# One register load for four tiles' expert numbers, and an earlier placing with scatters spread over the last sample

## The reference

```
s = _L0_attn_ref(xn, W_Q, b_Q, W_K, b_K, W_V, b_V, W_O, b_O, ln1_w, ln1_b, ln2_w, ln2_b)
g = _silu(_L0_ffn_ref(xn, Wr, br, W1, b1, g1, be1, W2, b2))   # router, top 2 of 16,
x = x + s * g                     # per expert: gelu(layernorm(h W1 + b1) g1 + be1) W2 + b2
```

## Time and profile before

| | |
|---|---|
| median of 3 runs | 1665.83 us |
| profiled execution | 1672.02 us |
| its span (first to last instruction) | 1670.1 us |
| busy in the span | PE 1285.4, DVE 1070.8, ACT 724.9, POOL 600.8 us |
| layer 0's attention, about | 42 to 567 us |
| its last sample, steps 0 to 31 | 426 to 561 us |
| its experts, about | 569 to 665 us |

### The profile page before, as it was taken

The page is one execution under the profiler, slowest core; times in us unless marked ns, Lnnn a source line. Parts: engine busy times, 40 slices in busy tenths (PEclk is TensorE's granted clock), DMA queues, the critical chain, the costliest instruction groups (busy, mean ns, idle before and its releaser), DMA issues. The chain is left out here.

```text
span 1670.1 us, 21792 instructions
## 1 busy us (share of the span) xinstructions
PE 1285.4 (77%) x7188; PEld 869.9 (52%) x7188; DVE 1070.8 (64%) x2574; ACT 724.9 (43%) x1526; POOL 600.8 (36%) x597
## 2 busy tenths in 40 slices
PE   1799999998987777376677985785784886788885
PEld 0355554654644555254564663553563465566664
DVE  1366676778686343455655995996897699724334
ACT  1345555455443234123236653662672573343332
POOL 1243444343338422422311442343243144225551
PEclk9998999999988678677778897797897799799998
DMA  7200000000000112430000000000000000001113
GB/s 176 71 1 1 1 1 2 1 1 1 1 4 29 51 51 70 129 111 13 13 1 1 1 1 0 1 1 0 1 1 1 1 1 1 26 12 34 35 33 89
DMA packets 54315, 40.36 MB, mean 24 GB/s; under 512 B 13175, under 2 KB 46685, under 8 KB 54205
## 3 DMA queue, kind: packets, MB, share of 16 engines
q1 hardware_dynamic: 35516, 23.91, 4.9%
q0 software_dynamic: 4544, 9.32, 2.0%
q10 hardware_dynamic: 14146, 5.75, 1.6%
HBM read 25.92 MB, written 13.04 MB: 23 GB/s over the span
## 5 line engine op out<-in xcount | busy, mean ns | idle before, releaser
L753 POOL TENSOR_TENSOR PR<-PR,R 128x256 f32<-128x256 f32 (+3 forms) x128 | 161.5, 1262 | 280.8 <-DVE R L1205 276.3
L1617 POOL TENSOR_TENSOR SA<-SA,H 128x512 f32<-128x512 f32 x64 | 81.8, 1277 | 258.2 <-DVE H L1844 258.2
L1839 DVE TENSOR_TENSOR_SCAN H<-DAS,H 128x512 f32<-128x512 f32 x128 | 174.6, 1402 | 0.0
L1022 ACT ACTIVATE PR<-banks,NM 128x129 f32<-128x129 f32 (+3 forms) x256 | 132.6, 527 | 47.5 <-DVE NM L1182 45.0
L415 PE MATMUL banks<-BCR,identR 96*128 96x512 f32 x256 | 110.7, 519 | 54.5 <-DVE H L1844 45.6
L415 PEld LDWEIGHTS banks<-we,HH 128*128 128x128 f32 x1024 | 145.3, 211 | 10.4
L415 PE MATMUL banks<-we,HH 128*128 128x128 f32 x1024 | 144.5, 294 | 0.0
L415 PEld LDWEIGHTS banks<-PTS,V 128*64 128x64 f32 x1280 | 72.9, 143 | 103.4 <-issue 97.1
L415 PE MATMUL banks<-XNT,we 128*128 128x512 f32 x256 | 120.7, 594 | 0.0
L415 PE MATMUL banks<-PTS,V 128*64 128x128 f32 x1280 | 105.0, 295 | 19.6 <-DVE PTS L1190 12.6
L1190 DVE COPY PTS<-banks 128x128 f32<-128x128 f32 (+3 forms) x128 | 62.2, 486 | 86.8 <-PE banks L893 83.8
(11 more groups left out here) (512 smaller groups left out, 2700.2 us busy)
## 6 DMA issues: line engine op xcount, KB each, us to landing
xsort<-zrow SPq DMA_DIRECT2D x1, 3072.0 KB, 13.1
XS<-xsort SPq DMA_DIRECT2D x12, 256.0 KB, 2.9
ysort<-PTS SPq DMA_DIRECT2D x12, 256.0 KB, 2.2
pj_stage<-in_L_ffn_w_proj SPq DMA_DIRECT2D x1, 2048.0 KB, 10.2
we<-in_L_ffn_we SPq DMA_DIRECT2D x1, 2048.0 KB, 9.3
we<-yrows SPq DMA_DIRECT2D x8, 256.0 KB, 4.9
X<-in_L_attn_resid_pre ACTq DMA_DIRECT2D x4, 256.0 KB, 4.7
xrows<-XN SPq DMA_DIRECT2D x4, 256.0 KB, 2.3
```

What stands on the lines that cost most here:

```text
L753: nc.gpsimd.tensor_tensor(p, p, R[:, n, :].unsqueeze(2).to_broadcast([P, 2, w]), ALU.mult).then_inc(pn, 1)
L1022: nc.scalar.activation(PR0[:, q % 2, s, OFF[t]:OFF[t] + w], ps2(n)[:, s, 0:w], ACT.Exp, bias=NM[:, n, s:s + 1], accum_out=L[:, n, s:s + 1] ...
L1617: nc.gpsimd.tensor_tensor(Y[m], Y[m], H[:, n % 2, m, :], ALU.add).then_inc(ya, 1)
L1839: nc.vector.tensor_tensor_scan(H[:, n % 2, m, :], DA[:, n % 4, m, :], H[:, n % 2, m, :], 0.0, ALU.mult, ALU.add).then_inc(scn, 1)
```

## The change

Three things, all in layer 0:

1. VectorE packs the four expert numbers of a unit into one integer (number i times 16 to the power i, summed), and TensorE loads this one per unit and takes each number out by shift and mask.
2. In the last sample "rank" comes first (step 1), "cc" at step 3, the four "o" at steps 5 to 11, "sel" at step 17. The placing parts 7 to 12 run at steps 3, 4, 6, 7, 9 and 11. The four parts of the output norm move three steps later (13, 14, 19, 20).
3. The 32 scatters are issued in steps 12 to 31, one or two each, instead of two in each of steps 16 to 31.

```
                     u = 2 * (i // T) + t // 2
                     key = None
-                    if u == 0 and b:
+                    if b == B - 1:
+                        if u == 0:
+                            key = ("rank",)
+                        elif u == 1:
+                            key = ("cc", b - 1)
+                        elif u < 6:
+                            key = ("o", b - 1, u - 2)
+                        elif u == 8:
+                            key = ("sel",)
+                    elif u == 0 and b:
                         key = ("cc", b - 1)
...
-                            if b and i == 11:
+                            late = 3 * (b == B - 1)
+                            if b and i == 11 + late:
                                 out_scale(b - 1)
-                            if b and i == 17:
+                            if b and i == 17 + late:
                                 out_norm(b - 1)
-                            if b == B - 1 and i >= 16:
-                                scatter(2 * (i - 16))
-                                scatter(2 * (i - 16) + 1)
+                            if b == B - 1 and i >= 12:
+                                for k in range(32 * (i - 12) // 20, 32 * (i - 11) // 20):
+                                    scatter(k)
...
+                                packed = nc.tensor.value_load(TEI[0:1, u:u + 1], min_val=0, max_val=E ** 4 - 1)
                                 for i in range(4):
-                                    e = nc.tensor.value_load(TEI[0:1, 4 * u + i:4 * u + i + 1], min_val=0, max_val=E - 1)
+                                    e = (packed >> (4 * i)) & (E - 1)
...
-                                nc.vector.tensor_scalar(TEI[:, :], TEF[:, :], float(E - 1), None, ALU.min).then_inc(el, 1)
+                                link(nc.vector.tensor_scalar(TEF[:, :], TEF[:, :], float(E - 1), None, ALU.min))
+                                link(nc.vector.tensor_tensor(TEP[:, :].rearrange("o (g i) -> o g i", i=4),
+                                                             TEF[:, :].rearrange("o (g i) -> o g i", i=4),
+                                                             radix[:, :].unsqueeze(1).to_broadcast([1, NF, 4]), ALU.mult))
+                                link(nc.vector.reduce_sum(TEF[:, 0:NF], TEP[:, :].rearrange("o (g i) -> o g i", i=4), AX.X))
+                                nc.vector.tensor_copy(TEI[:, :], TEF[:, 0:NF]).then_inc(el, 1)
 
-                        PLACE_AT = {12: (7,), 13: (8,), 14: (9,), 15: (10,), 16: (11,), 17: (12,)}
+                        PLACE_AT = {3: (7,), 4: (8,), 6: (9,), 7: (10,), 9: (11,), 11: (12,)}
...
+                        for i in range(4):
+                            last = nc.vector.memset(radix[:, i:i + 1], float(E ** i))
+                        link(last)
...
-                                if i == 10:
+                                late = 3 * (b == B - 1)
+                                if i == 10 + late:
                                     out_stats(b - 1)
-                                if i == 16:
+                                if i == 16 + late:
                                     out_apply(b - 1)
```

More of the change, by code:

```diff
@@ L603, in layer0 @@
                         key = ("w1", u - 1)
-                    elif b == B - 1:
-                        key = {5: ("rank",), 10: ("sel",)}.get(u)
                     elif u == 5:
@@ L665, in layer0 @@
                 TEF = sbr("TEF0", [1, 4 * NF], c=c)
-                TEI = sbr("TEI0", [1, 4 * NF], I32, c=c)
+                TEP = sbr("TEP0", [1, 4 * NF], c=c)
+                radix = sbr("radix0", [1, 4], c=c)
+                TEI = sbr("TEI0", [1, NF], I32, c=c)
                 EC = sbr("EC0", [E, 4], c=c)
```

## The result

The changed kernel takes 1637.2 us (median of 4 runs, 1635.88 to 1638.29) where the kernel before takes 1664.1 (1661.51 to 1669.95): a ratio of 0.9833, 95% interval 0.9804 to 0.9862. The forecast was 1640. The profiled execution has a time of 1637.49 us and a span of 1635.7, against 1672.0 and 1670.1 before. The profile of before is thus 7.9 us above the median of its runs and that of the changed kernel 0.3 us: the two profiles differ by 34.5 us, the medians by 26.9.

What follows compares the result with a forecast made beforehand. Bounds: TensorE early in the last sample, then VectorE's placing and GpSimd's scatters; in the experts, the cross-engine chain. Terms -17.3, +4.8 and -13.6 sum to -26.1: 1645.9 us profiled, 1640 median; own range 1631 to 1649, overall 1629 to 1658.

Steps and rivals of the forecast that it cites:

- Experts, forecast -17.3: Layer 0's expert layer, twelve units of four tiles: one load per unit saves 17.3 us, bounds 0 and -21.
- The pitch of the hidden products: Expert layer, time per tile's hidden product at full clock: falls from 0.76 to 0.27 to 0.30 us.
- The mean of the two clock levels: Expert layer: half the time at each clock level, periods 4.7 and 5.5 us, so 5.2 taken.
- The rival that register work is as dear as the loads: Expert layer: pitch stays at 0.7 or so, set by the number of register instructions; 1657 us, chance 0.09.
- chain close over another wait: Expert layer: ScalarE's in-order copies bind, period falls only to 6 us; -9 instead of -17.3, 1648 us, within a 0.15 case.
- A to C, forecast +4.8: Last sample, steps 0 to 11 in groups of four: early placing and ranks add 4.8 us, bounds 0 and +10.
- The new wait for "cc": Last sample, step 3: turned shares come later, VectorE waits with row maximum 3 queued behind; about 1.5 us.
- the slower rival: Last sample, steps 0 to 11: TensorE idles, its clock falls to the lower level; 1674 us, chance 0.05.
- D to H, forecast -13.6: Last sample, steps 12 to 31 in groups of four: 75.3 us against 88.9, bounds 0 and -19.
- GpSimd's need, as forecast: Last sample, steps 12 to 31: GpSimd's work per four-step group at 1.24 us a scatter, 11.3 to 16.4 us.
- The yardstick of 13.15 for a group: Sample 1 group with only two V products as spares, 13.15 us; over it steps 12 to 31 lose 23.1 us.
- The rival in which the early groups eat the scatters' gain: Last sample: steps 0 to 11 stretch by 10 us, later ones give 9; 1648 or 1649 us, within a 0.15 case.

Runs made afterwards that it cites:

- no_registers: Changed kernel with expert weights from fixed places, no register load, shifts, masks or address work (output differs): 1616.9 us, 0.9738 of the kernel before.
- load_only: Kernel before with the packed expert numbers alone (one load per unit), old order of the last sample: 1648.5 us, 0.9888 of the kernel before.
- cc_first: Changed kernel with turned first-row shares at step 1, ranks at step 3, placing parts 7, 8 and 10 a step later: 1630.0 us, 0.9824 of before.
- all_four: Changed kernel with load ahead of the waits, HN before statistics, scatters from step 8, and turned shares ahead of the ranks: 1611.5 us, 0.9718 of before.
- scatters_late: Changed kernel with two scatters in each of steps 16 to 31, as before the change: 1642.5 us, 0.9848 of the kernel before.
- all_three: Changed kernel with load ahead of the waits, HN before statistics, and scatters from step 8: 1612.8 us, 0.9719 of the kernel before.
- order_only: Changed kernel with one load per tile again and no packing, so only the last sample's order is new: 1658.1 us, 0.9941 of the kernel before.
- norm_late: Kernel before with only the four parts of the output norm three steps later in the last sample: 1666.5 us, 0.9985 of the kernel before.
- after_again: The changed kernel itself, unaltered, measured once more beside the last version on the same chip: 1632.7 us, 0.9839 of the kernel before.
- norm_first: Changed kernel with VectorE making HN of unit g-2 before the statistics of unit g-1: 1621.0 us, 0.9763 of the kernel before.

## Why the prediction was right, by its own steps

**Experts, forecast -17.3, measured -17.6.** The sum holds, and its parts too: nine periods 13.3 forecast, 13.5 measured; units 0, 1 and the last 4.0 forecast, 4.1 measured (35.0 to 30.9). But the period of 5.19 came out near the forecast's 5.2 by two errors that cancel. *The pitch of the hidden products* was the mis-sized term: 0.27 to 0.30 was forecast, four products 1.1 us; they take 1.47 at full clock. Shift and mask aren't free as the single address instruction of the earlier trace rows is; no_registers, with neither, has 1.13 us. So the full-clock period is 5.05, not 4.7. *The mean of the two clock levels* was the other: half of the time at each was read from a clock of 0.74, but the clock rose to 0.89, and six of the nine periods had full-clock products (6 x 5.05 + 5.35 + 5.51 + 5.52 = 46.7). Had it stayed, the period would have been (5.05 + 5.5) / 2 = 5.3 and this term 12.4 to 12.6.

The rival that register work is as dear as the loads is false: load_only has 78.4 us in the experts where before has 95.1. Nor did the chain close over another wait at 6 us a period. What was missed in this part is the bigger thing. The prediction took 1.05 us from HN to products as "semaphore, one load and register work" and kept it as given. It is 0.62 us of load that can stand ahead of the wait. The chain was read rightly, and a link of it was not questioned.

**A to C, forecast +4.8, measured +4.2.** A +1.86 and B +1.65 against 2 each, C +0.7. The new wait for "cc" is there:

```profile
437.47 0.17 DVE L1224 TENSOR_TENSOR CC<-PR,R 128x6 f32<-128x6 f32 x1 [1.48 <-PE banks L415]
...
440.28 1.92 PE L415 MATMUL banks<-X1T,WQ 128*128 128x512 f32 x2 [1.72 <-DVE G L1153]
...
443.27 1.62 DVE L1270 TENSOR_SCALAR CNT<-CNT 128x16 f32<-128x16 f32 x1
```

VectorE waits 1.48 us (forecast 1.5); cc_first, which takes it away, gives 1.9, though all_four got only 0.3 out of the same order. The rest of the sum is right by terms that are not: VectorE's busy time came out at 12.2, 14.4 and 12.8 us in A to C, where 14.2, 14.7 and 11.8 were forecast, so that A grew by 1.9 us with less work and more waiting than reckoned. The second row is the slower rival's mechanism, a TensorE that has idled and a product of 1.92 us: it occurs once in A, whose clock is 0.92, and B has 0.97, C 1.00; it never falls below the 0.9 named as the sign against. The third row is the small operation beside a GpSimd multiplication, 1.62 us for what takes 0.17 alone. The prediction took such a stall to be in part 7; it is in part 8 now. The four new small operations lie at 474.4 to 475.2, 0.7 us of VectorE, as forecast.

**D to H, forecast -13.6, measured -15.3.**

| | D | E | F | G | H |
|---|---|---|---|---|---|
| forecast | 13.4 | 15.4 | 17.6 | 15.2 | 13.7 |
| measured | 14.8 | 13.8 | 16.3 | 15.5 | 13.2 |
| GpSimd's need, as forecast | 11.3 | 13.7 | 16.4 | 13.7 | 12.5 |

The need at 1.24 us a scatter is what E and F take (13.8, 16.3), with nothing above it; the 1.2 to 1.7 that the forecast put on top there were not paid. D fails in the other direction, and scatters_late shows why: there a scatter costs by its place in the step, not by the engine's free time. G is 1.8 over its need with a granted clock of 0.83. In all_three G takes 12.1 us, at full clock and with three scatters fewer.

The yardstick of 13.15 for a group was too high. D of scatters_late, with the square-root step of the norm and some spares, takes 11.99, so the sum lost over it was underestimated. The rival in which the early groups eat the scatters' gain had +10 and -9 us; with +4.2 and -15.3 it is out.

**The signs named.** Period of 4.7 to 5.5: yes. A and B longer by 2: 1.9 and 1.7. First scatter at about 482: 479. E at 15 to 16: 13.8, better. A pitch of 0.27 without queue idle: no, 0.37. GpSimd never waiting 4 us for VectorE: true from the first scatter on, where the longest wait is 2.97. Ahead of that no: in A to C it waits up to 5.94 us, as it did before, with nothing else to do.

**The sum.** -26.1 forecast for the profiled execution, -34.5 measured between the two profiles, -27 between the medians. The stretches that the forecast spoke of give -28.6. The other 5.9 lie in the layers after, whose code is the same, and the prediction had put 0 there. So the profiled execution was missed by 8.4 us (1645.9 against 1637.5), and that the 1640 still came within 3 us of the median is in part luck: the prediction took off 6.2 us because the profile of before lay that far above the median of its first three runs, and the profile of the changed kernel lies only 0.3 above its own.

What the 5.9 us are stays open. One block of the first products after the experts, in before, in the changed kernel, and in the changed kernel measured again:

```profile
696.45 5.24 PE L415 MATMUL banks<-QK 128*128 128x512 f32 x8
```
```profile
666.93 3.70 PE L415 MATMUL banks<-QK 128*128 128x512 f32 x8
```
```profile
665.31 5.87 PE L415 MATMUL banks<-QK 128*128 128x512 f32 x8
```

Between the first two profiles the block and the two ahead of it, at a higher clock, make 2.6 of the 5.9 us. But the third has the changed kernel's code and before's slow block, so this difference is of the execution and not of the change. Over all of the layers after the experts a difference is left even so: the three profiles with a load per tile (before, order_only, norm_late) have 1004.9 to 1005.9 us, all eleven others 996.0 to 1001.9 (after_again 998.5). On one chip that ran both kinds it is 1004.9 twice against 1001.5 and 1001.9. A packed load that ended 30 us earlier as the cause of these 3 us is not shown.

## What to carry to other kernels

In a chain that goes over several engines, take every link apart, and ask of each instruction behind a wait whether it needs what is waited for: a register load that doesn't belongs ahead of the wait, and here that was worth 8 us where packing four loads in one was worth 17. Two halves of one engine's step that serve different units should stand in the order in which the next engine needs them. Work that is spread into an engine's gaps costs nothing only in the steps where that engine waits for others; the busy share of a group doesn't tell which these are. And before a forecast of a median is read as hit or missed, compare profile with profile too: an offset between profile and median need not be the same after the change.

## What the runs showed of the hardware

- A register load with its checks on TensorE's queue, behind a semaphore wait, holds the next product back by 0.62 us (1.00 against 0.38); ahead of the wait it is hidden. A shift and a mask cost about 0.1 us per product of 0.28, where the address instruction alone costs nothing (four products 1.06 us with it and without).
- The granted clock was higher in the kernels whose TensorE stood idle less between blocks. Over the experts it was 0.76 to 0.78 with a load per tile (three profiles), 0.83 to 0.91 with one load behind the waits (six profiles, of which the changed kernel itself has 0.88 and 0.83), 0.94 when the regular wait ahead of the products fell from 1.81 to 1.21 us, and 0.96 at 0.97 us. norm_first, with regular waits of 0.8 us and two over 2 us, has 0.91. So a wait taken out of the chain also took periods at the lower level away, which came to 0.9 us beside 5.6.
- A single idle time doesn't decide the clock: behind 1.38 us of it the same product took 1.13 us in cc_first and 1.97 in all_four, and in no_registers a block behind a wait of 2.30 us still ran at full clock (1.13 us).
- VectorE's small operation beside a GpSimd multiplication can be held until that ends, here ten times its time (1.62 against 0.17 us), and moving the code moves the victim. The operation of 443.27 ends at 444.89, the multiplication at 444.87:

```profile
442.97 1.90 POOL L762 TENSOR_TENSOR PR<-PR,R 128x1024 f32<-128x1024 f32 x1 [5.43 <-DVE R L1216]
```

In cc_first and all_four it is a small operation of part 7 (1.69 and 1.68 us), which ends 0.02 to 0.03 us after the multiplication. Not every operation is caught: the one at 443.06, inside the same multiplication, took its 0.17. The centring of the attention output, four operations, was another victim in the kernel before, 2.67 us; it is 1.27 now:

```profile
488.36 2.67 DVE L1172 TENSOR_SCALAR MT<-SA,mv,rc 128x128 f32<-128x128 f32 x4
```
```profile
501.88 1.27 DVE L1183 TENSOR_SCALAR MT<-SA,mv,rc 128x128 f32<-128x128 f32 x4
```
